# A row shuffled once with 66 columns on VectorE and copied on ScalarE, in place of a shuffle of 130 columns

## What is computed

```python
def step(buf, q_i):                                   # buf: the last 64 vectors, B x 64 x D
    ki = jnp.concatenate([buf, jnp.zeros((B, 1, D), feature.dtype)], axis=1)
    scores = jnp.einsum('bwd,d->bw', q_i[:, None, :] * ki, w2_w) + w2_b[0]
    alpha = jax.nn.softmax(scores, axis=1)            # over 65 entries
    v_i = jnp.einsum('bwd,bw->bd', ki, alpha)
    new_buf = jnp.concatenate([buf[:, 1:, :], v_i[:, None, :]], axis=1)
    return (new_buf, v_i)
_, vs = jax.lax.scan(step, init_buf, qs)              # 960 steps, one after the other
v_local = jnp.concatenate([feature[:, :W, :], jnp.transpose(vs, (1, 0, 2))], axis=1)
y = jnp.tanh(v_local) * feature + feature
```

## Time and profile before

| | |
|---|---|
| time, median of 3 runs (lowest to highest) | 2723.62 us (2720.71 to 2729.23) |
| the profiled execution: its own time, and its span | 2731.38 us, 2729.3 us |
| first layer's loop over chunks, from the first shuffle of a row | from 49.7 us to 1368.6 us of the span |
| busy share of the span: VectorE, ScalarE, TensorE, GpSimd | 79%, 49%, 43%, 17% |
| VectorE busy between 400 and 800 us | 376.43 of 400 us |
| ScalarE busy in the same stretch | 168.16 of 400 us |

### The profile page before, as it was taken

The page is one execution under the profiler, slowest core; times in us unless marked ns, Lnnn a source line. Parts: engine busy times, 40 slices in busy tenths (PEclk is TensorE's granted clock), DMA queues, the critical chain, the costliest instruction groups (busy, mean ns, idle before and its releaser), DMA issues. The chain is left out here.

```text
span 2729.3 us, 41936 instructions
## 1 busy us (share of the span) xinstructions
PE 1172.4 (43%) x7272; PEld 522.0 (19%) x7272; DVE 2157.0 (79%) x15955; ACT 1340.9 (49%) x3573; POOL 451.5 (17%) x1053
## 2 busy tenths in 40 slices
PE   2011010101010110101026777878877777778696
PEld 1000000000000000000011111224322333233365
DVE  6999999999999999999947898866776666865233
ACT  2343434444444434343322555658755775578642
POOL 0111111111111111111000110141024111311211
PEclk8555555555555555555566999889988988789898
DMA  5000000000000000000032031003120311001100
GB/s 144 1 4 3 5 3 5 4 4 5 3 5 3 5 3 5 3 5 5 2 79 39 1 78 32 13 16 100 24 46 19 89 44 33 22 19 35 34 1 24
DMA packets 82322, 65.85 MB, mean 24 GB/s; under 512 B 11838, under 2 KB 66920, under 8 KB 82056
## 3 DMA queue, kind: packets, MB, share of 16 engines
q1 hardware_dynamic: 78984, 56.89, 8.7%
q0 software_dynamic: 3072, 6.30, 0.7%
HBM read 34.77 MB, written 28.05 MB: 23 GB/s over the span
## 5 line engine op out<-in xcount | busy, mean ns | idle before, releaser
L1470 DVE TENSOR_REDUCE nm_half<-pair 128x2 f32<-128x1024 f32 x512 | 611.4, 1220 | 197.8 <-PE pair L1718 183.0
L342 ACT ACTIVATE ex<-row,nmax 128x65 f32<-128x65 f32 x960 | 336.1, 350 | 769.2 <-DVE row L408 676.7
L1358 ACT ACTIVATE pt<-pair 128x1024 f32<-128x1024 f32 x512 | 513.3, 1025 | 379.3 <-PE pair L1728 365.2
L403 DVE SCALAR_TENSOR_TENSOR junk<-ex,tab 128x65 f32<-128x65 f32 x2850 | 581.2, 229 | 1.9 <-issue 0.9
L523 PE MATMUL p_s<-tab,bdg 128*128 128x32 f32 x120 | 31.9, 406 | 769.2 <-DVE tab L408 769.2
L408 DVE SCALAR_TENSOR_TENSOR tab<-rz,raw 128x1 f32<-128x1 f32 (+1 forms) x1890 | 297.8, 158 | 10.9 <-ACT ex L342 5.5
L1694 PE MATMUL p_o<-pt,va 128*9 128x512 f32 x2048 | 296.1, 653 | 7.0 <-ACT pt L1358 7.0
L420 DVE STREAM_SHUFFLE row<-tab 128x130 f32<-128x130 f32 x930 | 274.8, 295 | 2.3 <-issue 2.1
L1718 PE MATMUL pair<-ks,qs 48*128 48x512 bf16 x1024 | 209.0, 419 | 112.8 <-ACT pt L1358 56.1
L403 DVE DVE_READ_ACCUMULATOR junk<-ex,tab 128x1 f32 x2850 | 233.1, 82 | 0.2
L1728 PE MATMUL pair<-qs,ks 50*128 50x512 bf16 x1024 | 210.1, 414 | 53.1 <-ACT pt L1358 23.8
(11 more groups left out here) (281 smaller groups left out, 2216.0 us busy)
## 6 DMA issues: line engine op xcount, KB each, us to landing
parts_dram<-parts SPq DMA_DIRECT2D x48, 256.0 KB, 3.5
qs<-parts_dram SPq DMA_DIRECT2D x32, 192.0 KB, 4.8
ks<-parts_dram SPq DMA_DIRECT2D x32, 192.0 KB, 5.3
hid<-xs_dram SPq DMA_DIRECT2D x33, 128.0 KB, 2.1
ys_dram<-hid SPq DMA_DIRECT2D x33, 128.0 KB, 1.8
x<-in_x SPq DMA_DIRECT2D x4, 512.0 KB, 8.5
w_W<-in_W SPq DMA_DIRECT2D x1, 2048.0 KB
w_W<-in_W SPq DMA_DIRECT2D x8, 256.0 KB
```

The source lines that it names most:

```text
L342: nc.scalar.activation(ex[:, r % 2, :], row[:, r % 2, 1, :], ACT.Exp, bias=nmax[:, r % 2:r % 2 + 1], accum_out=z[:, r % 2:r % 2 + 1]).then ...
L403: nc.vector.scalar_tensor_tensor(junk[:, g, :], ex[:, k, :], CAP, tab[:, g, r:r + ROW], ALU.min, ALU.mult, accum_out=raw[:, g:g + 1]).then ...
L1358: nc.scalar.activation(pt[:, kt % 2, :, tokens(t)], pair[fill.pair][:, :, :], ACT.Exp, scale=SCALE).then_inc(s_exp, 1)
L1470: nc.vector.reduce_max(nm_half[:, t, hp % 2, :, q], pair[fill.pair][:, :, :], AX.X, negate=True)\
```

## The change

The buffer `row` loses its second half and has 66 columns (ROW + 1) for each of its two places; a new buffer `row_exp` of 2 x 65 columns is what the exponential reads. The shuffle of line 420 moves 66 columns from column r-1 once. The sum for the next score reads its columns 0 to 64, the maximum its columns 1 to 65 (65 where it read 64). After each exponential but the last of a chunk ScalarE copies columns 1 to 65 of the next row into `row_exp`. The missing score now goes into `row_exp`; for this VectorE also waits for the copy (s_copy), and a second `sem_inc` stands ahead of that instruction to carry the further wait. A chunk's first exponential reads `row` itself.

```diff
-        row = sb("row", [P, 2, 2, ROW])
+        row = sb("row", [P, 2, ROW + 1])
+        row_exp = sb("row_exp", [P, 2, ROW])
...
-                    nc.scalar.activation(ex[:, r % 2, :], row[:, r % 2, 1, :], ACT.Exp, bias=nmax[:, r % 2:r % 2 + 1],
+                    nc.scalar.activation(ex[:, r % 2, :], (row_exp[:, r % 2, :] if r else row[:, 0, 1:]), ACT.Exp, bias=nmax[:, r % 2:r % 2 + 1],
                                          accum_out=z[:, r % 2:r % 2 + 1]).then_inc(s_exp, 1)
+                    if r < L - 1:
+                        act.wait_ge(s_row, L * c + r + 2)
+                        nc.scalar.copy(row_exp[:, 1 - r % 2, :], row[:, 1 - r % 2, 1:]).then_inc(s_copy, 1)
...
-                src = tab[:, 0, r:r + ROW]
-                pair = bass.AP(src.tensor, src.offset, [src.ap[0], [1, 2], [1, ROW]])
-                nc.vector.stream_shuffle(row[:, q % 2, :, :], pair, [q] * L).then_inc(s_row, 1)
+                nc.vector.stream_shuffle(row[:, q % 2, :], tab[:, 0, r:r + ROW + 1], [q] * L).then_inc(s_row, 1)
...
-                nc.vector.reduce_max(nmax[:, r % 2:r % 2 + 1], row[:, r % 2, 0, 1:], AX.X, negate=True)\
+                nc.vector.reduce_max(nmax[:, r % 2:r % 2 + 1], row[:, r % 2, 1:], AX.X, negate=True)\
...
-                        nc.vector.scalar_tensor_tensor(junk[:, 3, :], ex[:, k, :], CAP, row[:, 1 - k, 0, :], ALU.min,
+                        nc.vector.scalar_tensor_tensor(junk[:, 3, :], ex[:, k, :], CAP, row[:, 1 - k, 0:ROW], ALU.min,
...
                         dve.wait_ge(s_raw_new, m)
                         dve.sem_inc(s_pace, 1)
                         dve.wait_ge(s_rz, n + 1)
-                        divided(row[:, 1 - k, 1, WIN - 1:WIN].unsqueeze(2), 3, 4, k, s_new)
+                        dve.sem_inc(s_pace, 1)
+                        dve.wait_ge(s_copy, m)
+                        divided(row_exp[:, 1 - k, WIN - 1:WIN].unsqueeze(2), 3, 4, k, s_new)
```

More of the change, by code:

```diff
@@ L125, in window_attention @@
         s_raw, s_raw_score, s_score, s_raw_new = sem("s_raw"), sem("s_raw_score"), sem("s_score"), sem("s_raw_new")
-        s_clear = sem("s_clear")
+        s_clear, s_copy = sem("s_clear"), sem("s_copy")
         s_bdc, s_pv, s_vr, s_vall, s_pt, s_vt2, s_vt1, s_g, s_bdg = (
@@ L432, in _ @@
                 dve.sem_inc(s_pace, 1)
-                nc.vector.stream_shuffle(row[:, 0, 1, :], tab[:, 0, 0:ROW], [0] * L).then_inc(s_row, 1)
+                nc.vector.stream_shuffle(row[:, 0, 1:], tab[:, 0, 0:ROW], [0] * L).then_inc(s_row, 1)
                 shifted(1, 0)
                 dve.wait_ge(s_row, L * c + 1)
-                nc.vector.reduce_max(nmax[:, 0:1], row[:, 0, 1, :], AX.X, negate=True).then_inc(s_max, 1)
+                nc.vector.reduce_max(nmax[:, 0:1], row[:, 0, 1:], AX.X, negate=True).then_inc(s_max, 1)
                 dve.wait_ge(s_bdc, c + 1)
```

## The result

The changed kernel takes 2772.67 us (median of 4 runs, 2765.67 to 2780.48) against 2724.23 (4 runs, 2720.71 to 2729.23): ratio 1.0177, interval 1.0146 to 1.0209. It is 48 us slower, outside the range of 2708 to 2742, on the side of the rival that I gave 0.20 and put at 2738 us.

The account below looks back on a forecast made before the run. It took the loop between ScalarE's exponential and VectorE's work behind it as the bound, the shuffle hidden. Terms -2 - 1.8 + 0.9 + 0 + 0 + 0 = -2.9 us gave 2720.7 us; range 2708 to 2742.

Parts of the forecast that it names:

- the rival that I gave 0.20: Second counting instruction, between maximum and missing score, lengthens the chain by +9 to +26 us: 2738 us, chance 0.20.
- The exponential's loop bounds the step, and the shuffle is hidden.: Plain step of 1.24 us: coefficients wait for the exponential, not the shuffle, hidden by 0.04 us; narrowing gains nothing there.
- The rival that VectorE's queue is the bound: VectorE's own queue sets the step; 64 columns fewer give 0.065 us in 870 steps: 2665 us, chance 0.07.
- Late steps and chunk starts, -2 and -1.8 us.: Narrower shuffle: some 94 late steps gain 0 to 6 us, taken as -2; 30 chunk starts gain 0.06 each, -1.8.
- The copy, 0.: ScalarE's copy behind each exponential, 0.25 us long, ready 0.12 to 0.22 us before the missing score needs it: cost 0.
- The side jobs behind it: ScalarE's side jobs and GpSimd's work behind them start some 0.2 us later: 6 us either way, taken as 0.
- The second counting instruction, taken at 0.05 us and hidden: 0.: Added sem_inc before the missing score: between 0 and 0.09 us, taken as 0.05, inside the room, so 0 us.
- The room: Slack before the missing score behind the first counting instruction: 0.19 - 0.13 = 0.06 us, with 0.02 more before the exponential.
- The price: Cost of the second counting instruction, its semaphore long set so never stood upon: 0 to 0.09 us, taken as 0.05.
- The rule of the sequencer: Skill page: control instructions take sequencer time whatever their semaphore; at 50 to 100 ns, hidden or up to 17 to 35 us.
- The marks I had named: Signs of the costly counting instruction: maximum to score above 0.14 us, score more than 0.22 behind line 450's accumulator.
- the marks for "right": Step 1.24 us, coefficients 0.47 behind exponential, VectorE gap before them, shuffle about 231 ns, VectorE's busy time down 50 to 60 us.

Follow-up runs that it names:

- experiment 7: Kernel before with the narrow shuffle alone, no copy, the missing score written into the one buffer: 2715.62 us, ratio 0.9951.
- experiments 9 and 10: VectorE's step reordered, no counting instruction before the score: from the changed kernel 2705.50 us (0.9932), from the kernel before, wide shuffle, 2780.82 us (1.0199).
- experiment 8: Kernel before with only ScalarE's copy added behind each exponential, into a buffer nobody reads, wide shuffle: 2715.96 us, ratio 0.9949.
- experiments 2 and 3: Kernel before with one more sem_inc before the missing score, 2774.29 us (1.0198), and with two more, 2855.58 us (1.0495).
- experiment 5: Changed kernel without the second sem_inc, a bare wait instruction standing in its place: 2729.81 us, ratio 1.0032 to the kernel before.
- b1: Kernel before with one more sem_inc in front of the missing score, no copy, wide shuffle: 2774.29 us, ratio 1.0198.
- b2: Kernel before with two more sem_incs in front of the missing score: 2855.58 us, ratio 1.0495.
- experiment 1: Changed kernel with one counting instruction before the score again, the maximum carrying the wait for the reciprocal: 2708.71 us, ratio 0.9952 to the kernel before.
- i1: The run of experiment 5: changed kernel with a bare wait instruction instead of the second sem_inc, 2729.81 us, ratio 1.0032.
- h1: Narrow shuffle without copy, VectorE's step reordered with the maximum one step ahead, one counting instruction before the shuffle: 2695.82 us, 0.9889 to the kernel before.
- h1d: As h1, but the shuffle carries its wait itself, without the counting instruction: 2637.57 us, ratio 0.9682 to the kernel before.
- c1: The run of experiment 8: kernel before with only ScalarE's copy added, 2715.96 us, ratio 0.9949.

## Why the prediction was wrong

- *The exponential's loop bounds the step, and the shuffle is hidden.* Right. 0.47 us from exponential to coefficients before and after the earlier trace rows, and the narrow shuffle alone left the step at 1.24 us (experiment 7). The rival that VectorE's queue is the bound gave 2665 us for it; it took 2716. Where VectorE is the bound (experiments 9 and 10), 64 columns cost 0.07 us a step, as it had them.
- *Late steps and chunk starts, -2 and -1.8 us.* The boundary went from 3.46 to 3.39 us, 30 x 0.07 = 2.1. The narrow shuffle by itself gives 14 us; my bound for it, 6.1 + 1.8, lies at the lower end of its interval of 8 to 19. (The late steps are 921 - 825 = 96 and not 94, which changes nothing.)
- *The copy, 0.* Right: it lasts 0.246 us (I took 0.25), begins 0.51 behind the exponential and ends 0.35 ahead of the score in the rows above. The side jobs behind it, which I took at 0 and at most 6 us either way, gained 13 us where the copy stood alone (experiment 8), and nothing in the changed kernel: its longer steps are 65 us for 62.
- *The second counting instruction, taken at 0.05 us and hidden: 0.* This is the step that failed, in two of its numbers. The room: I put the first instruction at 0.13 us from the wait's end, by the coefficients in the earlier trace rows. That wait is carried by a bare wait instruction, the one in front of the score by a sem_inc. By experiments 2 and 3 it is 0.17 there, and the 0.04 between them is what experiment 5 measured for the counting up; so the room was 0.03 and not 0.06. The price: I argued that an instruction whose semaphore is set costs less than one on which the queue stands, and took half. It costs 0.09 in full (b1 to b2), the upper end. 0.17 + 0.09 - 0.20 = 0.06, less 0.02 of room in front of the exponential (it begins 0.03 behind the score's end in the median of the steps, where it was 0.05), plus 0.01 by which the score's record is longer (0.16 for 0.15), makes the 0.05 us a step. With my own upper bound of 0.03 the rival could reach 2720.7 + 26 = 2747; the measured chain is 0.02 beyond it, because the room was mis-sized as well.
- *The rule of the sequencer.* The Trainium skill's page "Advanced Engine Details and Errata", section "Sequencer Loop", says that the sequencer executes control instructions itself. b1 and b2 agree: an instruction that nothing holds costs its 0.09 us all the same. The same page of the Trainium skill gives, in "Network/Comms", 50 to 100 ns for reading a semaphore value from the sequencer. The 0.09 us of a sem_inc lie in it, and the 0.05 of the bare wait lie at its lower end; no run here shows that it is the same thing. From my own rows I had a full price of 0.09 us, if by a misread one, and gave it too little weight against a chance of 0.57.
- *The marks I had named.* More than 0.14 us from the maximum's start to the score's, with the score more than 0.22 behind line 450's accumulator: this named the case, and both came, 0.19 and 0.26. Of the marks for "right" the 0.47 us, the mean of the shuffle, the 930 copies and the earlier maximum came. The plain step did not stay at 1.24 us, VectorE's busy time did not fall with the shuffle's, and there is no idle gap in front of the coefficients: the shuffle begins at 725.01 and ends at 725.23, when they have begun.

## What to carry to other kernels

In a loop between two engines at a pace of a microsecond, count the instructions that only wait or count as well as those that compute. The slack in front of each instruction on the closed chain is what decides, and a wait that needs an instruction of its own to carry it can cost more than the columns that the change saves. Before a wait is added, see whether an instruction further ahead in the queue can carry it, because it has no wait or one that repeats an earlier one, as in experiment 1. And read the price of such a carrier from a row with the same kind of instruction; if there is none, keep the upper end and let it weigh in the chances.

## What the runs showed of the hardware that I had not expected

A sem_inc that carries a wait costs 0.09 us on VectorE's queue even when nothing holds it (0.26 to 0.35 us, b1 to b2), a bare wait instruction in its place 0.04 less (i1). The shuffle can carry its wait itself, and takes 0.05 us off the step by it (h1 to h1d). Work of GpSimd that meets VectorE costs different amounts depending on which instruction it meets: the step took 1.94 us where it met the missing score, and 1.61 where it met a sum behind it and then the coefficients (before and c1).
